# Edge stages of a graph network: sums over groups of 128 edges in place of 256, and a walk table of three rows

## The chip, the cores and the metric

The kernel runs on one core of a Trainium2 chip. The metric is the device time of one execution in microseconds (us). Engines in the text: TensorE (PE; PEld is its weight load), VectorE (DVE), ScalarE (ACT), GpSimd (POOL), SyncE (SP). Line numbers (L1213) are those of the kernel before.

## The reference, cut to what matters

The input is a graph of 6250 nodes with 256 features and 200,000 edges, sorted by their target `dst`. Three graph-attention layers run one after the other. Two other parts, a linear-attention mixer and a mixture of experts, complete the model; the change does not touch them.

```python
xh = (h @ W).reshape(n, heads, d)
a_s = (xh * att_src).sum(-1)
a_d = (xh * att_dst).sum(-1)
alpha = leaky_relu(a_s[src] + a_d[dst], 0.2)
amax = segment_max(alpha, dst, num_segments=n)
e = exp(alpha - amax[dst])
z = segment_sum(e, dst, num_segments=n)
out = segment_sum(xh[src] * (e / z[dst])[:, :, None], dst, num_segments=n)
h = relu(layernorm(out + bias) (+ h))
```

For every edge a row of its source node is fetched, weighed with a softmax over all edges of the same target, and added to the target's row.

## The kernel before, in words

**The walk** (`prepare_walk`) runs once. It cuts the sorted edges into groups and the nodes into 49 blocks of 128 (`NB`). A step of the walk is one pair of a group of edges and a block of nodes: a group whose targets lie in two blocks is visited twice. With groups of 256 edges (`GE`) there are 782 groups (`TG`) and 782 + 48 steps. For each step the walk finds which group it is (`grp`, by counting on TensorE how many groups the walk has passed), fetches the group's targets, the following edge's targets and the sources with three indirect DMAs per 128 steps (L297, L299, L301), and makes from them: `srcT` (source index of every edge), `relT` (the target's place in its block), `lastT`, the masks and links for the segment maximum (`lanes`, `links`), `powers`, and `words`, in which the block numbers of a window are packed.

**Edge stages** (`edge_phase`) run three times, between node stages that compute `rows`, the 260 values per node which the edges fetch. An edge stage goes over windows of `WS` = 20 lanes, and a lane is 128 edges. Before, a window is `WG` = 10 groups of 256 edges, and there are 83 windows (`NW`). The windows are written out one after the other, not looped. What happens to window w is spread over several steps of a software pipeline. In the step n each engine runs a fixed list:

- POOL gathers the 20 lanes of a window, one indirect DMA for 128 edges (L1213), up to four windows ahead (`RING`); before it writes chunk k of a buffer it waits until the sums of that chunk, four windows back, are done.
- PE: sums of window n, between them the `distances` of window n+3; then `spread_fade` (n+1), `turn` (n+2), more sums, `spread_ad` (n+3), the last sum, the mixer's matmuls, and `turn_back` (n+2).
- DVE: `differences` and `tops` (n+1), `sum_ad`, `sum_scores` and `leak` (n+2; `sum_scores`, L1565, waits for the window's last gather), then `fade_sums` and the `add`s of window n (L1684), and between these adds the `weigh`s (L1666) and `onehots` (L1658) of window n+1, and the two scans and what belongs to them for window n+2. `scan_on` (L1579) waits for PE's `turn` and ACT's `fade`.
- ACT: `exponentials` (n+1), five copies of one-hot chunks (n+3, L1263), `fades` (L1251), the mixer's functions, and `load_node` (L1232), which copies one small tile per group.

The sum of a group is two matmuls, one per lane, added up in one PSUM bank; DVE then adds the bank to the block's row of `acc`. Three banks are in use:

```python
wait_past(pe, added, WG * w + g + 1 - since_bank(g))
for j in range(2):
    mm = pe.matmul(ps_o[BANK_OF[g]][:, 0:GW], OH[:, 2 * g + j, :], G[n][:, 2 * g + j, :],
                   start=(j == 0), stop=(j == 1))
mm.then_inc(summed, 1)
```

The add waits for the add before it, as both may go to the same block, and its address comes from a register:

```python
v.wait_ge(summed, WG * w + g + 1)
v.wait_ge(added, WG * w + g)
a = acc[:, bass.ds(b, 1), :].rearrange("p a c -> p (a c)")
v.tensor_tensor(a, a, ps_o[BANK_OF[g]][:, 0:GW], ALU.add).then_inc(added, 1)
```

The block b comes from `blocks_of` (L1106): a word is loaded into a register, and each next block adds one bit of it. The mixer's 49 tiles run beside the first 49 to 55 windows of each edge stage.

## Time and profile before

| what | us |
|---|---|
| median of 3 runs | 7659.41 (7658.97 to 7662.24) |
| the profiled execution | 7658.34 |
| its span, first to last instruction | 7656.4 |
| walk, up to the node stage's first DMA | 124.0 |
| edge stage 0, first to last sum_scores | 2056.5 |
| edge stage 1, the same | 2054.4 |
| edge stage 2, the same | 2055.1 |

The busy time of an engine counts its own instructions, not those of its sequencer (waits, register work). Idle time is put down to what ended it. The rest of the span is node stages, a final stage and the experts.

### The profile page before, as it was taken

What the parts mean: (1) busy time and instruction counts of PE and PEld (TensorE: products, weight loads), DVE (VectorE), ACT (ScalarE), POOL (GpSimd) and SP (SyncE); (2) the same over time, 40 slices, a digit from 0 to 9 for tenths busy, and PEclk for the clock granted to TensorE, in tenths of its full rate; (3) what the DMA queues carried; (4) which work ended last, traced back from release to release, by engine and by line L of the source; (5) the groups of instructions that cost most, each with busy time, mean ns of one, the idle gap of its engine ahead of it and who ended that gap; (6) DMA issues with size and microseconds to landing.
All of it is one profiled execution on the core that took longest, in us unless ns stands there. A gap on an engine that the chain in (4) does not pass through costs nothing. (4 is left out here: it accounts for less than half of the span.)

```text
span 7656.4 us, 113586 instructions
## 1 busy us (share of the span) xinstructions
PE 5492.3 (72%) x23859; PEld 3669.8 (48%) x23860; DVE 5058.0 (66%) x13667; ACT 2558.7 (33%) x7905; POOL 5156.8 (67%) x5441
## 2 busy tenths in 40 slices
PE   3587777777776577777777776577878877673498
PEld 1354454444444355555544444355555544442397
DVE  4466666666667577777776667577777776668643
ACT  1322222222222333334332223244444432223465
POOL 1577777777774677777777773677777777771443
PEclk8777877877767677777777767687787777776699
DMA  4555555554543444444444444444444444444444
GB/s 121 157 145 142 143 145 141 145 139 136 140 138 102 119 120 123 121 123 123 122 116 112 112 110 122 120 123 129 129 126 129 127 119 111 112 110 142 131 71 92
DMA packets 547591, 955.11 MB, mean 125 GB/s; under 512 B 126946, under 2 KB 380876, under 8 KB 546827
## 3 DMA queue, kind: packets, MB, share of 16 engines
q0 software_dynamic: 260256, 692.79, 34.5%
q1 hardware_dynamic: 283451, 253.69, 11.0%
q8 instruction: 177, 2.90, 0.2%
q14 instruction: 411, 3.37, 0.1%
q10 hardware_dynamic: 3296, 2.36, 0.1%
HBM read 801.28 MB, written 155.92 MB: 125 GB/s over the span
## 5 line engine op out<-in xcount | busy, mean ns | idle before, releaser
L1213 POOL DMA_INDIRECT edges_G<-rows,edges_index x4980 | 4721.0, 948 | 1661.9 <-issue 1482.3
L1425 PE MATMUL edges_ps_o<-edges_G,edges_OH 128*128 128x264 f32 x9960 | 3561.9, 508 | 1200.2 <-DVE acc L1684 1197.0
L1425 PEld LDWEIGHTS edges_ps_o<-edges_G,edges_OH 128*128 128x128 f32 x9960 | 2319.0, 250 | 1989.8 <-DVE acc L1684 1367.0
L1263 ACT ACTIVATE edges_OHT<-edges_ps_far 128x512 bf16<-128x512 f32 x1245 | 740.9, 595 | 2299.6 <-PE edges_ps_far L1385 2299.5
L1666 DVE TENSOR_TENSOR edges_G<-edges_G,edges_ps_c 128x1024 f32<-128x1024 f32 x1245 | 1503.2, 1208 | 0.0
L1684 DVE TENSOR_TENSOR acc<-acc,edges_ps_o 128x264 f32 x2490 | 1060.1, 426 | 299.3 <-DVE acc L1684 162.2
L1565 DVE TENSOR_TENSOR edges_tu<-edges_ad,edges_G 128x80 f32<-128x80 f32 x249 | 75.1, 301 | 1255.5 <-DMA edges_G<-rows,edges_index 1255.5
L1385 PE MATMUL edges_ps_far<-edges_rels,pole_rows 5*128 5x512 bf16 x1245 | 618.8, 497 | 344.4 <-ACT edges_OHT L1263 301.8
L1658 DVE TENSOR_TENSOR edges_OH<-edges_ps_c,relT 128x512 f32<-128x512 f32 x1245 | 846.0, 680 | 0.6 <-ACT edges_ps_c L1240 0.5
L1385 PEld LDWEIGHTS edges_ps_far<-edges_rels,pole_rows 5*128 5x128 bf16 x1245 | 117.6, 94 | 976.8 <-issue 497.6
L1232 ACT ACTIVATE edges_node<-terms 128x12 bf16 x2490 | 476.1, 209 | 143.2 <-issue 89.0
L1240 ACT ACTIVATE edges_ps_c<-edges_diff 128x80 f32<-128x80 f32 x249 | 60.0, 241 | 1108.4 <-DVE edges_diff L1646 1107.2
L1579 DVE TENSOR_TENSOR_SCAN edges_run<-edges_masks,edges_ps_s 128x128 f32<-128x128 bf16 x249 | 104.8, 421 | 378.4 <-ACT edges_fade L1251 374.3
L2467 POOL DMA_INDIRECT x<-experts_Y,experts_token x105 | 165.1, 1572 | 252.5 <-DMA x<-experts_Y,experts_token 215.9
L1340 ACT ACTIVATE edges_xh<-edges_R,edges_mshift,edges_mscale 128x256 f32<-128x256 f32 x98 | 58.8, 600 | 574.2 <-DVE edges_mshift L1732 574.2
L2039 POOL DMA_INDIRECT xslot<-final_XH,final_slots x98 | 100.4, 1025 | 173.1 <-DVE final_slots L2219 145.1
L2493 PEld LDWEIGHTS experts_psH<-experts_xs,experts_Wup 128*128 128x128 f32 x1680 | 206.3, 194 | 5.3
L2493 PE MATMUL experts_psH<-experts_xs,experts_Wup 128*128 128x128 f32 x1680 | 206.7, 277 | 0.0
L2502 PE MATMUL experts_psY<-W,experts_hT 128*128 x840 | 198.7, 380 | 0.1
L895 PE MATMUL node_psB<-node_Wx,node_hT 128*128 128x264 f32 x588 | 192.8, 460 | 0.0
L1375 PEld LDWEIGHTS edges_ps_s<-edges_node,edges_OHT 128*128 128x128 bf16 x4980 | 161.2, 96 | 53.0 <-issue 10.9
L1375 PE MATMUL edges_ps_s<-edges_node,edges_OHT 128*128 128x12 bf16 x4980 | 161.9, 168 | 12.3 <-DVE edges_run L1579 10.2
(360 smaller groups left out, 6057.8 us busy)
## 6 DMA issues: line engine op xcount, KB each, us to landing
edges_G<-rows,edges_index POOLq DMA_INDIRECT x4980
xslot<-edges_blank SPq DMA_DIRECT2D x80, 650.0 KB
edges_masks<-lanes SPq DMA_DIRECT2D x249, 96.0 KB
rows<-node_ext SPq DMA_DIRECT2D x147, 130.0 KB, 2.3
experts_X<-xslot SPq DMA_DIRECT2D x105, 130.0 KB, 2.1
node_rows<-rows SPq DMA_DIRECT2D x98, 130.0 KB, 2.2
h<-node_Hn SPq DMA_DIRECT2D x98, 128.0 KB, 1.7
W<-in_L_ffn_W SPq DMA_DIRECT2D x16, 512.0 KB
```

The source lines that it names most:

```text
L895: pe.matmul(psB[slot % 2][:, 0:RW + H], hT[:, slot % TILE_RING, k, :], Wx[:, k, :], start=(k == 0), stop=False)
L1213: g.indirect_dma_start(G[n][:, s, 0:RW], None, dr["rows"], bass.IndirectOffsetOnAxis(index[n][:, s:s + 1], 0)).then_inc(gathered[n], 16)
L1232: ins = a.activation(node[n][:, g, :], terms[:, bass.ds(b, 1), :, :].rearrange("p a h k -> p (a h k)"), ACT.Copy)
L1263: a.activation(OHT[:, 4 * k:4 * k + 4, :].rearrange("p s e -> p (s e)"), ps_far[:, :], ACT.Relu, bias=1.0, scale=-1.0).then_inc(oht_ready, 1)
L1375: mm = pe.matmul(ps_ad[:, s * KEPT:(s + 1) * KEPT], OHT[:, s, :], node[n][:, s // 2, :], start=True, stop=True)
L1385: pe.matmul(ps_far[:, :], pole[r, :], rels[r, 4 * k * P:4 * (k + 1) * P], start=True, stop=True).then_inc(far_ready, 1)
L1425: mm = pe.matmul(ps_o[BANK_OF[g]][:, 0:GW], OH[:, 2 * g + j, :], G[n][:, 2 * g + j, :], start=(j == 0), stop=(j == 1))
L1658: v.tensor_tensor(OH[:, 4 * k:4 * k + 4, :], ps_iota.unsqueeze(1).broadcast_to([P, 4, P]), rel.unsqueeze(2).broadcast_to([P, 4, P]), ALU.i ...
L1666: v.tensor_tensor(g4[:, :, :, 0:D], g4[:, :, :, 0:D], ps_w[:, 4 * k:4 * k + 4, :].unsqueeze(3).broadcast_to([P, 4, H, D]), ALU.mult).then_ ...
L1684: v.tensor_tensor(a, a, ps_o[BANK_OF[g]][:, 0:GW], ALU.add).then_inc(added, 1)
L2493: mm = pe.matmul(psH[slot % 2][:, c * P:(c + 1) * P], Wup[:, slot % 2, k, c * P:(c + 1) * P], xs[:, slot % 2, k, :], start=(k == 0), stop= ...
L2502: mm = pe.matmul(psY[slot % 2][:, 0:C], hT[:, slot % 2, c * P:(c + 1) * P], W2[:, bass.ds(e, 1), c, :].rearrange("p a o -> p (a o)"), star ...
```

## The change

A group becomes one lane of 128 edges. There are now 1563 groups, 1563 + 48 steps of the walk and 81 windows of 20, so 1620 lanes a stage instead of 1660. Each lane has its own matmul pair with start and stop, its own bank in turn, its own add and its own block, taken from two words a window. `load_node` copies 20 tiles instead of 10. The DVE list holds the adds two at a time where it held one, and four between the first two weighs.

The walk is written anew: one DRAM table of three rows per group (targets, following targets, sources) is made straight from the inputs by DMAs on ACT's queue, and one indirect DMA fetches all three rows for 128 steps. The last targets are loaded from the input itself. The group numbers come as a row and are turned by 13 small matmuls. Links, masks and powers go out in 4 DMAs instead of 43, and `powers` lies step by step in DRAM.

```diff
 H = 4
 D = C // H
 RW = C + H
-GE = 2 * P
+GE = P
 GW = RW + H
 TG = -(-E // GE)
-WG = 10
-WS = 2 * WG
-NW = -(-(TG + NB - 1) // WG)
-NG = NW * WG
+WS = 20
+HG = WS // 2
+NW = -(-(TG + NB - 1) // WS)
+NG = NW * WS
 LANES = 32
 POLE = 5
...
+        triples = dr["triples"]
+        sources = ((dst, 0), (dst, 1), (src, 0))
...
+            full = (TC - 1) * P
+            sp.dma_start(dstI[:, 0:TC - 1, :], dst[0:full * GE].rearrange("(c p e) -> p c e", p=P, e=GE)).then_inc(dst_in, 16)
             sp.wait_ge(pool, 1)
-            full = (TC - 1) * P
-            sp.dma_start(dstI[:, 0:TC - 1, :], dr["dst_pad"][0:full, :].rearrange("(c p) e -> p c e", p=P)).then_inc(dst_in, 16)
-            sp.dma_start(dstI[0:pad_rows - full, TC - 1, :], dr["dst_pad"][full:pad_rows, :]).then_inc(dst_in, 16)
+            sp.dma_start(dstI[0:whole - full, TC - 1, :], dst[full * GE:whole * GE].rearrange("(p e) -> p e", e=GE)).then_inc(dst_in, 16)
+            sp.dma_start(dstI[whole - full:whole - full + 1, TC - 1, 0:rest], dst[whole * GE:E].rearrange("(a e) -> a e", a=1)
+                         ).then_inc(dst_in, 16)
...
+        @block.scalar
+        def _(a):
+            for m, (of, o) in enumerate(sources):
+                a.dma_start(triples[0:whole, m, :], of[o:o + whole * GE].rearrange("(t e) -> t e", e=GE)).then_inc(edges_in, 16)
+            for m, (of, o) in enumerate(sources):
+                a.dma_start(triples[whole:TG, m, 0:rest - o], of[o + whole * GE:E].rearrange("(a e) -> a e", a=1)).then_inc(edges_in, 16)
+            a.wait_ge(pads_set, 2)
+            a.dma_start(triples[TG:pad_rows, :, :], pad[:, :, :]).then_inc(edges_in, 16)
+            for m, (of, o) in enumerate(sources):
+                a.dma_start(triples[whole:TG, m, rest - o:P], pad[:, m, rest - o:P]).then_inc(edges_in, 16)
+            a.wait_ge(lanes_ready, 3)
+            a.dma_start(dr["lanes"].rearrange("(c p) x -> p c x", p=P), lanes[:, :, :, :].rearrange("p c m e -> p c (m e)")
+                        ).then_inc(walk_out, 16)
+            a.wait_ge(powers_ready, 3)
+            a.dma_start(dr["powers"].rearrange("(c p) k e -> p c (k e)", p=P), powers[:, :, :, :].rearrange("p c k e -> p c (k e)")
...
+            g.wait_ge(edges_in, 16 * 10)
             g.wait_ge(index_ready, 1)
             for c in range(GC):
-                g.indirect_dma_start(Dg[:, c, :, :].rearrange("p a b -> p (a b)"), None, dr["dst_pad"],
-                                     bass.IndirectOffsetOnAxis(grpI[:, c:c + 1], 0)).then_inc(dst_rows, 16)
-                g.indirect_dma_start(Ng[:, c, :, :].rearrange("p a b -> p (a b)"), None, dr["dst_next"],
-                                     bass.IndirectOffsetOnAxis(grpI[:, c:c + 1], 0)).then_inc(next_rows, 16)
-                g.indirect_dma_start(Sg[:, c, :, :].rearrange("p a b -> p (a b)"), None, dr["src_pad"],
-                                     bass.IndirectOffsetOnAxis(grpI[:, c:c + 1], 0)).then_inc(src_rows, 16)
+                g.indirect_dma_start(Tg[:, c, :, :].rearrange("p a b -> p (a b)"), None, triples.rearrange("t a b -> t (a b)"),
+                                     bass.IndirectOffsetOnAxis(grpI[:, c:c + 1], 0)).then_inc(rows_in, 16)
 
...
+                    v.tensor_copy(st[t][:, c * P:c * P + n], ps_tr[:, c % 3, m * P:m * P + n]).then_inc(copied, 1)
+            v.wait_ge(copied, 3 * GC)
 
         @block.tensor
         def _(pe):
             pe.wait_ge(iotas, 8)
             for c in range(TC):
                 pe.wait_ge(compared, c + 1)
-                for r in range(2):
-                    pe.matmul(ps_row[:, r, 0:rowT], ones[:, :], passed[:, c, r * rowT:(r + 1) * rowT],
-                              start=(c == 0), stop=(c == TC - 1))
-            for m in range(GC):
-                for c in range(TC):
-                    mm = pe.matmul(ps_col[:, m:m + 1], passed[:, c, m * P:(m + 1) * P], ones[:, 0:1],
+                for r in range(QUARTERS):
+                    mm = pe.matmul(ps_row[:, r, 0:rowT], ones[:, :], passed[:, c, r * rowT:(r + 1) * rowT],
                                    start=(c == 0), stop=(c == TC - 1))
             mm.then_inc(walked, 1)
+            pe.wait_ge(row_ready, 1 + QUARTERS)
+            for m in range(GC):
+                mm = pe.matmul(ps_col[:, m:m + 1], row_grp[:, m * P:(m + 1) * P], st["ident"][0:1, 0:1], start=True, stop=True)
+            mm.then_inc(row_turned, 1)
+            pe.wait_ge(index_ready, 1)
+            pe.wait_ge(ends_ready, 2)
+            for m in range(2):
+                mm = pe.transpose(ps_col[0:GC, (1 + m) * P:(2 + m) * P], edge_ends[:, m, :], st["ident"][:, :])
+            mm.then_inc(ends_turned, 1)
             pe.wait_ge(rows_ready, 3)
...
@@ -925,13 +894,12 @@
     srcT, relT, lastT, words = (st[n] for n in ("srcT", "relT", "lastT", "words"))
     pole = st["pole"]
     BANKS = 3
-    BANK_OF = (0, 1, 2, 0, 1, 2, 0, 1, 2, 1)
-    CHUNKS = WG // 2
+    CHUNKS = WS // 4
     KEPT = 3 * H
     with Phase(nc, f"edges{layer}") as ph:
         G = [ph.sb(f"G{r}", [P, WS, GW]) for r in range(RING)]
         index = [ph.sb(f"index{r}", [P, WS], I32) for r in range(RING)]
-        node = [ph.sb(f"node{r}", [P, WG, KEPT], BF16) for r in range(RING)]
+        node = [ph.sb(f"node{r}", [P, WS, KEPT], BF16) for r in range(RING)]
         masks = ph.sb("masks", [P, RING, 1 + 3 * P], BF16)
         links = ph.sb("links", [P, RING, 2, WS], BF16)
...
 
             return not isinstance(i, int) or 0 <= RING * i + n + k < NW
 
-        def since_bank(g):
-
-            return next(d for d in range(1, WG + 1) if BANK_OF[(g - d) % WG] == BANK_OF[g])
+        def bank(w, g):
+            return ps_o[(WS * w + g) % BANKS][:, 0:GW]
 
         def blocks_of(eng, w):
 
-            word = eng.value_load(words[0:1, bass.ds(w, 1)], min_val=0, max_val=64 * 2 ** (WG - 1) - 1)
-            b = eng.snap(word & 63)
-            for g in range(WG):
-                b = nc.s_assert_within(b, 0, NB - 1, skip_runtime_bounds_check_because=ROWS_SEEN)
-                yield b
-                if g < WG - 1:
-                    b = eng.snap(b + ((word >> (6 + g)) & 1))
+            for half in range(2):
+                word = eng.value_load(words[0:1, bass.ds(2 * w + half, 1)], min_val=0, max_val=64 * 2 ** (HG - 1) - 1)
+                b = eng.snap(word & 63)
+                for g in range(HG):
+                    b = nc.s_assert_within(b, 0, NB - 1, skip_runtime_bounds_check_because=ROWS_SEEN)
+                    yield b
+                    if g < HG - 1:
+                        b = eng.snap(b + ((word >> (6 + g)) & 1))
 
         @block.sync
         def _(sp):
@@ -1132,7 +1100,7 @@
                 if w > 1:
                     wait_apart(sp, far_ready, FAR * (w - 1), passed_sp)
                 r = LANES * (w % 2)
-                sp.dma_start(rels[r:r + 3, :], dr["powers"][:, bass.ds(w * WS * P, WS * P)]).then_inc(rels_in[w % 2], 16)
+                sp.dma_start(rels[r:r + 3, :].rearrange("k (v e) -> k v e", e=P), dr["powers"][bass.ds(w * WS, WS), :, :].rearrange("v k e -> k v e")).then_inc(rels_in[w % 2], 16)
 
...
@@ -1372,7 +1340,7 @@
                 wait_past(pe, ad_ready, w)
                 wait_past(pe, ran, w)
                 for s in range(WS):
-                    mm = pe.matmul(ps_ad[:, s * KEPT:(s + 1) * KEPT], OHT[:, s, :], node[n][:, s // 2, :], start=True, stop=True)
+                    mm = pe.matmul(ps_ad[:, s * KEPT:(s + 1) * KEPT], OHT[:, s, :], node[n][:, s, :], start=True, stop=True)
                 mm.then_inc(ad_spread, 1)
 
                 for g in groups:
                     if g == 0:
                         pe.wait_ge(topped, w + 1)
-                    if g % 2 == 0:
-                        pe.wait_ge(oh_ready, CHUNKS * w + g // 2 + 1)
-                        pe.wait_ge(weighed, CHUNKS * w + g // 2 + 1)
-
-                    wait_past(pe, added, WG * w + g + 1 - since_bank(g))
-                    for j in range(2):
-                        mm = pe.matmul(ps_o[BANK_OF[g]][:, 0:GW], OH[:, 2 * g + j, :], G[n][:, 2 * g + j, :],
-                                       start=(j == 0), stop=(j == 1))
-                    mm.then_inc(summed, 1)
+                    if g % 4 == 0:
+                        pe.wait_ge(oh_ready, CHUNKS * w + g // 4 + 1)
+                        pe.wait_ge(weighed, CHUNKS * w + g // 4 + 1)
+
+                    wait_past(pe, added, WS * w + g + 1 - BANKS)
+                    pe.matmul(bank(w, g), OH[:, g, :], G[n][:, g, :], start=True, stop=True).then_inc(summed, 1)
 
             SPLITS = 3 - layer
 
@@ -1497,7 +1462,7 @@
                 here = exists(i, n)
                 for g in range(FAR):
                     if here:
-                        sums(i, n, [g])
+                        sums(i, n, (2 * g, 2 * g + 1))
                     if exists(i, n, 3):
                         distances(*later(i, n, 3), g)
...
@@ -1505,11 +1470,11 @@
                 if exists(i, n, 2):
                     turn(*later(i, n, 2))
                 if here:
-                    sums(i, n, range(5, 9))
+                    sums(i, n, range(10, 18))
                 if exists(i, n, 3):
                     spread_ad(*later(i, n, 3))
                 if here:
-                    sums(i, n, range(9, 10))
+                    sums(i, n, range(18, 20))
                 if mix:
                     mixes(i, n)
...
 
             def onehots(i, n, k):
                 w = RING * i + n
 
-                wait_past(v, summed, WG * (w - 1) + 2 * k + 2)
-                rel = relT[:, bass.ds(w * WG + 2 * k, 2), :].rearrange("p g j -> p (g j)")
+                wait_past(v, summed, WS * (w - 1) + 4 * k + 4)
+                rel = relT[:, bass.ds(w * WS + 4 * k, 4)]
                 v.tensor_tensor(OH[:, 4 * k:4 * k + 4, :], ps_iota.unsqueeze(1).broadcast_to([P, 4, P]),
                                 rel.unsqueeze(2).broadcast_to([P, 4, P]), ALU.is_equal).then_inc(oh_ready, 1)
 
@@ -1669,19 +1634,19 @@
             def fade_sums(i, n, b):
                 w = RING * i + n
                 v.wait_ge(fade_ready, w + 1)
-                wait_past(v, added, WG * w)
+                wait_past(v, added, WS * w)
                 a = acc[:, bass.ds(b, 1), 0:RW].rearrange("p a (h f) -> p (a h) f", h=H)
                 v.tensor_tensor(a, a, fade[:, :].unsqueeze(2).broadcast_to([P, H, D + 1]), ALU.mult).then_inc(faded, 1)
 
             def add(i, n, g, b):
                 w = RING * i + n
-                v.wait_ge(summed, WG * w + g + 1)
+                v.wait_ge(summed, WS * w + g + 1)
                 if g == 0:
                     v.wait_ge(faded, w + 1)
                 else:
-                    v.wait_ge(added, WG * w + g)
+                    v.wait_ge(added, WS * w + g)
                 a = acc[:, bass.ds(b, 1), :].rearrange("p a c -> p (a c)")
-                v.tensor_tensor(a, a, ps_o[BANK_OF[g]][:, 0:GW], ALU.add).then_inc(added, 1)
+                v.tensor_tensor(a, a, bank(w, g), ALU.add).then_inc(added, 1)
 
             def sum_kv(t):
...
                     fade_sums(i, n, b)
                     next(extra, None)
                     add(i, n, 0, b)
+                    add(i, n, 1, next(blocks))
                     next(extra, None)
-                    add(i, n, 1, next(blocks))
+                    for g in (2, 3):
+                        add(i, n, g, next(blocks))
                 if one:
                     weigh(*next1, 0)
                 next(extra, None)
                 if here:
-                    add(i, n, 2, next(blocks))
+                    for g in (4, 5):
+                        add(i, n, g, next(blocks))
                     next(extra, None)
-                    add(i, n, 3, next(blocks))
+                    for g in (6, 7):
+                        add(i, n, g, next(blocks))
                 if one:
                     weigh(*next1, 1)
                     onehots(*next1, 0)
@@ -1804,12 +1773,14 @@
                 if two:
                     scan_on(*next2)
                 if here:
-                    add(i, n, 4, next(blocks))
+                    for g in (8, 9):
+                        add(i, n, g, next(blocks))
                 next(extra, None)
                 if two:
                     scan_back(*next2)
                 if here:
-                    add(i, n, 5, next(blocks))
+                    for g in (10, 11):
+                        add(i, n, g, next(blocks))
                 if two:
                     turn_edges(*next2)
...
```

The parts left out rename semaphores and tiles of the walk, drop the second lane's index from its tiles, and repeat the pairing of the adds to the end of the list.

## Rows read from the trace of the kernel before

**Rows 1.** The page, part 1: busy time, share of the span and instructions of each engine.

```profile
PE 5492.3 (72%) x23859; PEld 3669.8 (48%) x23860; DVE 5058.0 (66%) x13667; ACT 2558.7 (33%) x7905; POOL 5156.8 (67%) x5441
```

**Rows 2.** Windows of the three stages, POOL's L1213: the row of their sum.

```profile
sum 6165.94, POOL 4660.16; mean POOL 1553.39
```

**Rows 3.** The page, part 5: xcount | busy, mean ns of one | idle before, releaser.

```profile
L1213 POOL DMA_INDIRECT edges_G<-rows,edges_index x4980 | 4721.0, 948 | 1661.9 <-issue 1482.3
...
L1425 PE MATMUL edges_ps_o<-edges_G,edges_OH 128*128 128x264 f32 x9960 | 3561.9, 508 | 1200.2 <-DVE acc L1684 1197.0
...
L1684 DVE TENSOR_TENSOR acc<-acc,edges_ps_o 128x264 f32 x2490 | 1060.1, 426 | 299.3 <-DVE acc L1684 162.2
```

**Rows 4.** Waits of DVE: 780:1481, 3050:3751, 5343:6044, 1684:2260, whole span (us, times, longest).

```profile
DVE edges_tu L1565 <- DMA edges_G<-rows,edges_index: 140.7, 28, 6.2
...
DVE edges_tu L1565 <- DMA edges_G<-rows,edges_index: 134.6, 29, 5.7
...
DVE edges_tu L1565 <- DMA edges_G<-rows,edges_index: 107.4, 28, 5.2
...
DVE edges_tu L1565 <- DMA edges_G<-rows,edges_index: 118.0, 23, 6.2
...
DVE edges_run L1579 <- ACT edges_fade L1251: 374.3, 242, 2.3
```

**Rows 5.** Timeline of DVE, stage 0: start us, us, instruction, [idle before <-releaser].

```profile
1308.69 0.43 DVE L1684 TENSOR_TENSOR acc<-acc,edges_ps_o 128x264 f32 x1
1309.85 0.43 DVE L1684 TENSOR_TENSOR acc<-acc,edges_ps_o 128x264 f32 x1 [0.73 <-DVE acc L1684]
1310.20 1.22 DVE L1666 TENSOR_TENSOR edges_G<-edges_G,edges_ps_c 128x1024 f32<-128x1024 f32 x1
```

**Rows 6.** Timeline of DVE, end of stage 0: the second to the fourth of ten adds.

```profile
2369.98 0.43 DVE L1684 TENSOR_TENSOR acc<-acc,edges_ps_o 128x264 f32 x1 [0.38 <-PE edges_ps_o L1425]
2370.79 0.43 DVE L1684 TENSOR_TENSOR acc<-acc,edges_ps_o 128x264 f32 x1 [0.38 <-DVE acc L1684]
2371.59 0.43 DVE L1684 TENSOR_TENSOR acc<-acc,edges_ps_o 128x264 f32 x1 [0.37 <-DVE acc L1684]
```

**Rows 7.** L1106 by source: times in ns, min/median/max.

```profile
L1106 DVEq TENSOR_LOAD <-words x249: 299/303/559, 329.2 to 6927.8; - x125
L1106 DVEq FUSED_REGOPS  x249: 190/197/210, 329.8 to 6928.1; - x125
```

**Rows 8.** Timeline of PE, stage 0, one window.

```profile
1311.76 2.13 PE L1425 MATMUL edges_ps_o<-edges_G,edges_OH 128*128 128x264 f32 x4
1313.83 0.60 PE L1385 MATMUL edges_ps_far<-edges_rels,pole_rows 5*128 5x512 bf16 x1
...
1321.29 1.16 PE L1425 MATMUL edges_ps_o<-edges_G,edges_OH 128*128 128x264 f32 x4 [0.59 <-DVE acc L1684]
1322.28 0.39 PE L1466 MATMUL edges_ps_r<-edges_v,edges_high 128*128 128x130 f32 x2
...
1324.89 0.27 PE L1401 MATMUL edges_ps_s<-ident,edges_greatest 128*128 128x128 f32 x1
```

**Rows 9.** Timeline of ACT, the same window.

```profile
1315.43 0.26 ACT L1251 ACTIVATE edges_fade<-edges_ps_s,edges_front 128x4 f32<-128x4 f32 x1 [0.37 <-PE edges_ps_s L1393]
...
1317.32 2.41 ACT L1232 ACTIVATE edges_node<-terms 128x12 bf16 x10 [0.49 <-issue]
```

**Rows 10.** Timeline of the walk, all engines.

```profile
10.19 0.41 SPq L231 DMA_DIRECT2D walk_dstI<-dst_pad  x1
...
21.79 5.01 PE L405 MATMUL walk_ps_row<-walk_passed,walk_ones 128*128 128x415 bf16 x14 [21.79 <-DVE walk_passed L328]
...
28.79 1.16 POOL L297 DMA_INDIRECT walk_Dg<-dst_pad,walk_grpI  x1 [23.67 <-DVE walk_grpI L332]
...
96.23 16.46 SPq L263 DMA_DIRECT2D links<-walk_links  x28
124.03 0.34 SPq L573 DMA_DIRECT2D node_X<-in_x  x1
```

More of the change, by code:

```diff
@@ L354, in _ @@
-            ch.add(v.tensor_copy(Nf[:, :, :, :], Ng[:, :, :, :]))
-            v.tensor_copy(Sf[:, :, :, :], Sg[:, :, :, :]).then_inc(rows_ready, 1)
-            ch.wait()
-            for c in range(GC):
-                ch.add(v.tensor_scalar(rel[:, c, :, :], Df[:, c, :, :], blk[:, c:c + 1], float(2 * P - 1), ALU.subtract, ALU.min))
-            ch.wait()
-            v.tensor_scalar(rel[:, :, :, :], rel[:, :, :, :], -1.0, None, ALU.max).then_inc(rows_ready, 1)
-            v.tensor_tensor(last[:, :, :, :], Df[:, :, :, :], Nf[:, :, :, :], ALU.not_equal).then_inc(rows_ready, 1)
@@ L1823, in step @@
                 if here:
-                    add(i, n, 6, next(blocks))
+                    for g in (12, 13):
+                        add(i, n, g, next(blocks))
                 if two:
@@ L1827, in step @@
                 if here:
-                    add(i, n, 7, next(blocks))
+                    for g in (14, 15):
+                        add(i, n, g, next(blocks))
                 if two:
@@ L1839, in step @@
                 if here:
-                    add(i, n, 8, next(blocks))
+                    for g in (16, 17):
+                        add(i, n, g, next(blocks))
                 if one:
@@ L1843, in step @@
                 if here:
-                    add(i, n, 9, next(blocks))
+                    for g in (18, 19):
+                        add(i, n, g, next(blocks))
                 for _ in extra:
```

228 lines of the change are left out of this document (94 added, 134 removed).

## The prediction

> **What bounds the kernel now.** I began with the page's busy shares [rows 1]: TensorE, VectorE and GpSimd are busy for two thirds to three quarters, so they don't tell which one sets the pace. The stretches of the three edge stages do [rows 2]. From the first to the last sum_scores (L1565) the stages take 6165.94 us for 3 x 82 windows: 25.06 us a window. POOL's gathers [rows 3] are 20 a window, 0.948 us each with 0.30 us of issue between two (1482.3 us over 4980), 20 x 1.25 = 25.0 us. So GpSimd's gathers are the period, in all three stages.
>
> VectorE is next. In each window it stands still at sum_scores until the window's last gather has landed [rows 4]: 140.7/28 = 5.0 us a window in the part of stage 0 that also mixes, 134.6/29 = 4.6 in stage 1, 107.4/28 = 3.8 in stage 2, 118.0/23 = 5.1 once the 49 mixing tiles are done. Taken from 25.06 that leaves VectorE's own path: 20.0, 20.4, 21.2 and 19.9 us. This slack, 3.8 to 5.1 us, is what the change may spend for nothing.
>
> **Fewer windows.** 256-edge groups give 782 + 48 = 830 groups, 83 windows of 10. 128-edge groups give 1563 + 48 = 1611, so 81 windows of 20. Two windows a stage go, 40 gathers: if the period stayed, 6 x 25.06 = 150 us less.
>
> **Ten more adds a window.** A window still has 20 pairs of matmuls, but every one ends its own sum, so the add to acc (L1684) comes 20 times instead of 10. One add is 426 ns [rows 3], but its price depends on its neighbour. Behind an add, an independent instruction starts 0.35 us later (1309.85 to 1310.20), while an add behind an add starts far later, with the idle time put down to acc itself [rows 5]. It waits for the add before it, and then its block address is worked out. At the stage's end ten stand in a row, the second to the fourth at 2369.98, 2370.79 and 2371.59: 0.80 us apart, 0.38 of it idle [rows 6]. The new order puts the adds in pairs and, between weigh 0 and weigh 1, in a four. Each of the ten new ones has another add just in front, so I take 10 x 0.80 = 8.0 us. Bounds: 10 x 0.35 = 3.5 if their waits cost nothing, and 10 x 1.16 = 11.6 by the slowest pair shown (1308.69 to 1309.85).
>
> The Trainium skill ("VectorE: DVE Perf Modes", section "The DRAIN you can't avoid") speaks against this price: eight copies with a semaphore after each took as long as eight with one at the end, so a semaphore costs nothing extra there. By that rule the ten adds cost little over 3.5 us. The trace disagrees for this dependent add: 0.80 against 0.35 us [rows 5, 6].
>
> **The second word of blocks.** Twenty blocks need two words, so before add 10 there is a second load and decode on VectorE's sequencer: 0.303 + 0.197 = 0.50 us [rows 7]. scan_back, and the wait for add 9, cover part. I take 0.3 us a window, bounds 0 and 0.6.
>
> **What TensorE and ScalarE do to VectorE then.** scan_on waits for the fade, on average 374.3/242 = 1.55 us a window [rows 4]. The fade comes from PE behind sums and distances. Before, PE needed only add 1 for the last distance; now it needs add 6 (three banks, and sum 9 is in front of distance 4). From add 6 to the fade PE has about one sum, a distance, the fade matmul and a transpose. At the slow clock that is 1.07 (2.13 for two sums), 1.60 from the last distance's start to the fade's (1313.83 to 1315.43) and the fade's own 0.26: 2.9 us. At the fast clock a sum is 0.58 (1.16 for two) [rows 8, 9]. VectorE arrives there about 2.4 us after add 6 (add 7, a 1.13 us weigh, a 0.6 us one-hot). If sum 7 and distance 3 are still queued, another 2 us come on top. I keep half of the wait: -0.8 us; bounds: -1.55 (all gone) and +1.0.
>
> At the step's end, sum 19 needs add 16, and behind it on PE stand the mixes and turn_back, for which the next step's differences wait. From the start of the mixes at 1322.28 to turn_back at 1324.89 are 2.6 us [rows 8], plus a sum before and 0.27 after: 3.5 us. VectorE has add 17, weigh 4, two adds and a one-hot in that time, also about 3.5 us. I take 0.3 us where the window mixes and none later; bounds 0 and 1.5.
>
> **The edits with no price.** ScalarE copies 20 node blocks instead of 10: 2.41 us more a window [rows 9], of an engine busy for 33% of the span [rows 1], and the copies come last in its step; if that idle time went, 2.4 us would stand ahead of the next exponentials. The powers now come as 60 pieces of 256 bytes, not 3 rows: SP asks for them a window ahead. OH, weigh, gathers and matmuls stay 20 a window.
>
> **The new period.** Own path + 8.0 + 0.3 - 0.8 + 0.3 gives 27.8 us in stage 0, 28.2 in stage 1, 29.0 in stage 2. Where nothing mixes it is 19.9 + 8.0 + 0.3 - 0.8 = 27.4. All are over 25.06: VectorE becomes the bound, the 4 us of slack are gone, and POOL waits for sums.
>
> Per stage there are 80 periods after: two before any add, at 25.06, then 49 mixing and 29 without. Sum over stages: 49 x (27.84 + 28.22 + 29.02) = 4169; 3 x 29 x 27.43 = 2386; 6 x 25.06 = 150; together 6706. Before: 6166. That is +540. Behind the last sum_scores three steps with adds remain, which no gather covered before: 3 x 3 x (8.0 - 0.8) = +65.
>
> **The walk.** Before, it ends at 124.03 [rows 10]. Its chain: copies to DRAM until SP's load of dst at 10.19, the search, 21 gathers from 28.79 on, VectorE's work on the tables, then 28 small DMAs on SP from 96.23 (16.46 us) whose last landing the end awaits. After: dst is loaded at once (-9). The search is longer, 52 matmuls for 14 that took 5.01 us, so +14 at 0.36 us each, and some 2 us of turning the row. Only 13 gathers follow, -10 us at 1.25. VectorE casts three tables less, -3. The 28 DMAs become 2 and go out earlier, about -24 with their landing. The sum is -32 us; bounds -50 and -5, as the copies of the table now run beside the load of dst, and no row shows that.
>
> **Sum.** The profiled execution took 7658.34 us (span 7656.4 and 1.9 around it), 1.1 less than the median. 7658.3 + 540 + 65 - 32 = 8231; I say **8230 us**, 7% slower.
>
> **Rivals.**
> *A, the gathers stay the bound.* The new adds find cover, as the skill's rule would have it: 10 x 0.35 = 3.5 us is under the slack of 3.8 to 5.1, the period stays 25.06; it decides below 0.38 to 0.5 us for each added add. Then 7658 - 150 (six windows) + 32 (nine uncovered last steps of 3.5) - 32 = 7508 us. For it: an instruction that isn't an add does start 0.35 us behind one [rows 5]. Against it: [rows 6]. Chance 0.10.
> *B, the ring of three banks.* With one sum a bank PE runs three matmuls ahead, no longer six. If PE stays at the slow clock because it stops at so many adds, sum 7, distance 3 and sums 8 and 9 come in series behind add 4 and hold scan_on back 2.1 us, and the mixes come 1.2 us late. The period is then up 2.4 us from mine: 8230 + 234 x 2.4 = 8790 us. For it: PE already waited 1197 us for acc [rows 3], and after such a wait two sums took 2.13 us instead of 1.16 [rows 8]. Against it: PE had a wait of 5 us there, which VectorE's own wait for gathers made, and that wait goes. Chance 0.08.
>
> **Numbers.** Mine 0.80, A 0.10, B 0.08, and 0.02 for something between the old time and mine. The range: 0.95 us less a period over 234 periods (most of the fade's wait gone) gives 8008, 1.2 us more 8511; 8000 to 8520. Less than 0.2% either way is no change that can be told here. Faster is A, 0.10; same 0.01, from what lies between; slower 0.89.
>
> **What would show it.** Right: sum_scores no longer waits for a gather; the tables show POOL idle for about 2.5 us a window, released by ps_o; 4860 adds of about 0.43 us, second ones 0.8 us behind the first; periods of 27.4 to 29.0 us, the longest in stage 2; the node stage starts near 92 us. Wrong: a period of 25.0 with sum_scores still waiting for gathers (A), or scan_on and the adds waiting for PE for over 4 us a window (B). If the second of a pair starts under 0.5 us after the first, the price of the add is the step that failed.

## The result and the profile after

The changed kernel took **8515.07 us** (8503.82 to 8519.34, 4 runs) beside 7659.19 for the kernel before (7658.87 to 7662.24): a ratio of 1.1115, 95% interval 1.1100 to 1.1131. It is 856 us slower; the forecast was 571 slower (8230) in a range of 8000 to 8520. The direction and the bound that changes were right. A third of the added time was not foreseen, and the time lies inside the range by only 5 us.

The page after, part 1 and the lines that answer to [rows 1, 3]: xcount | busy, mean ns of one | idle before, releaser.

```profile
PE 6287.8 (74%) x23459; PEld 3582.0 (42%) x23460; DVE 6025.0 (71%) x15855; ACT 3055.0 (36%) x10215; POOL 5029.6 (59%) x5312
...
L1181 POOL DMA_INDIRECT edges_G<-rows,edges_index x4860 | 4602.5, 947 | 2545.6 <-issue 2078.7
L1392 PE MATMUL edges_ps_o<-edges_G,edges_OH 128*128 128x264 f32 x9720 | 4322.9, 566 | 1613.5 <-DVE acc L1649 1593.9
...
L1649 DVE TENSOR_TENSOR acc<-acc,edges_ps_o 128x264 f32 x4860 | 2076.0, 427 | 1358.4 <-DVE acc L1649 849.9
```

A gather costs what it did (947 ns), but the idle time before POOL's gathers went from 1661.9 to 2545.6 us. The add costs what it did too (427 ns). There are 2370 more of them, and the idle time in front of them grew from 299.3 to 1358.4 us. This idle time, 1059 us more, and the adds' own busy time, 1016 us more, together use up the 4 to 5 us a window in which VectorE had waited for gathers, and then lengthen the window. The busy shares hide it: DVE shows 71%.

VectorE's waits after, whole span (us in total, times, longest), to be held against [rows 4]:

```profile
DVE acc L1649 <- DVE acc L1649: 849.9, 2224, 0.7
DVE acc L1649 <- PE edges_ps_o L1392: 412.5, 757, 1.6
DVE edges_run L1544 <- ACT edges_fade L1219: 201.5, 147, 2.4
...
DVE edges_diff L1611 <- PE edges_ps_s L1369: 142.8, 87, 3.3
...
DVE edges_tu L1530 <- DMA edges_G<-rows,edges_index: 70.7, 6, 12.9
...
DVE edges_xh L1703 <- ACT edges_ps_c L1208: 31.3, 29, 1.1
...
DVE edges_den L1662 <- ACT edges_ps_c L1208: 30.4, 41, 1.1
```

sum_scores (now L1530) waited for a gather in every window; now it does so 6 times in the whole kernel. In its place stand five waits: the add for the add before it, the add for its sum, scan_on (L1544) for the fade, the differences (L1611) for turn_back, and, in the last two rows, the mixer's first instruction of a step for ScalarE's exponentials (L1208). The first needs no other engine. The next three come from TensorE, the fade by way of ScalarE. The last, 61.7 us in all, doesn't occur in the kernel before: there VectorE's wait for the gathers gave ScalarE the time.

VectorE's timeline in stage 0, as [rows 5]: start us, us, instruction, [idle before <-releaser].

```profile
1299.81 0.43 DVE L1649 TENSOR_TENSOR acc<-acc,edges_ps_o 128x264 f32 x1
1300.62 0.43 DVE L1649 TENSOR_TENSOR acc<-acc,edges_ps_o 128x264 f32 x1 [0.38 <-DVE acc L1649]
1301.43 0.43 DVE L1649 TENSOR_TENSOR acc<-acc,edges_ps_o 128x264 f32 x1 [0.38 <-DVE acc L1649]
1302.23 0.43 DVE L1649 TENSOR_TENSOR acc<-acc,edges_ps_o 128x264 f32 x1 [0.37 <-PE edges_ps_o L1392]
1302.58 1.21 DVE L1631 TENSOR_TENSOR edges_G<-edges_G,edges_ps_c 128x1024 f32<-128x1024 f32 x1
```

Adds behind adds start 0.80 to 0.81 us apart; the weigh behind the last starts after 0.35. So the dependent add has the price that the forecast took from [rows 6]. For eight copies the Trainium skill ("VectorE: DVE Perf Modes", section "The DRAIN you can't avoid") says that a semaphore after each costs nothing extra. This trace disagrees for the dependent add, 0.80 against 0.35 us.

Windows of the three stages, first to last sum_scores, POOL alone (us, busy, PEclk, DMA share, GB/s), as [rows 2]:

```profile
241.58:2546.91 2305.33, 1510.81 (x1595) 0.68 0.44 123
2788.90:5090.22 2301.32, 1510.31 (x1596) 0.73 0.38 103
5356.05:7735.44 2379.39, 1510.75 (x1596) 0.72 0.38 102
sum 6986.04, POOL 4531.87; mean POOL 1510.62
```

6986.04 against 6165.94 us: +820 for 240 periods instead of 246. From the last sum_scores of a stage to the first of the next it is 28.4 and 27.6 us more than before, and 21.9 more to the end: +78. The first sum_scores comes 37 us earlier. Together 820 + 78 - 37 = 861, which is the difference of the spans (8517.2 and 7656.4).

The periods, in the mean of the windows, with the same of the kernel "banks of pairs" below (us):

| windows | forecast | changed kernel | banks of pairs |
|---|---|---|---|
| mixing, stage 0 | 27.8 | 29.0 | 26.6 |
| mixing, stage 1 | 28.2 | 29.6 | 28.1 |
| mixing, stage 2 | 29.0 | 30.9 | 28.5 |
| the rest, stages 0, 1, 2 | 27.4 | 28.9, 27.8, 28.2 | 26.5, 26.7, 26.7 |

TensorE in the same stage, pieces of its timeline:

```profile
1311.37 2.13 PE L1392 MATMUL edges_ps_o<-edges_G,edges_OH 128*128 128x264 f32 x4 [0.29 <-DVE acc L1649]
1314.85 3.01 PE L1392 MATMUL edges_ps_o<-edges_G,edges_OH 128*128 128x264 f32 x6 [1.36 <-DVE acc L1649]
...
1320.34 0.71 PE L1392 MATMUL edges_ps_o<-edges_G,edges_OH 128*128 128x264 f32 x2 [0.87 <-DVE acc L1649]
...
1323.60 1.06 PE L1392 MATMUL edges_ps_o<-edges_G,edges_OH 128*128 128x264 f32 x4
```

The granted clock of these four stretches (us; busy and count of PE and PEld; PEclk, DMA share, GB/s):

```profile
1311.37:1313.50 2.13, 2.12 (x4) 1.07 (x4) 0.50 0.52 168
1314.85:1317.86 3.01, 3.01 (x6) 1.65 (x6) 0.50 0.42 115
1320.34:1321.05 0.71, 0.71 (x2) 0.29 (x2) 1.00 0.33 100
1323.60:1324.66 1.06, 1.06 (x4) 0.58 (x4) 1.00 0.36 114
```

TensorE does a few sums, stops for an add, does a few more. Two sums take 2.13 us at a granted clock of 0.50 (its lower level, 1.2 GHz) and 1.06 us at 1.00 (2.4 GHz), after the mixes, where it had run without a stop. A stop alone doesn't settle the level: the sum at 1320.34 also stands behind one and runs at 1.00. 9720 matmuls were busy for 4322.9 us, 9960 for 3561.9 before; the mean granted clock of the whole run is 0.72 against 0.75.

### The profile page after: what moved, and what is told of

Read it like the earlier page. It is cut to its first block and busy times, and to the rows that moved or that the text cites. A ratio compares the mean times of both kernels' runs of the same rounds, so it can differ in the third digit from the quotient of the medians.

```text
span 8517.2 us, 134431 instructions
## 1 busy us (share of the span) xinstructions
PE 6287.8 (74%) x23459; PEld 3582.0 (42%) x23460; DVE 6025.0 (71%) x15855; ACT 3055.0 (36%) x10215; POOL 5029.6 (59%) x5312
## 5 line engine op out<-in xcount | busy, mean ns | idle before, releaser
L1181 POOL DMA_INDIRECT edges_G<-rows,edges_index x4860 | 4602.5, 947 | 2545.6 <-issue 2078.7
L1392 PE MATMUL edges_ps_o<-edges_G,edges_OH 128*128 128x264 f32 x9720 | 4322.9, 566 | 1613.5 <-DVE acc L1649 1593.9
L1392 PEld LDWEIGHTS edges_ps_o<-edges_G,edges_OH 128*128 128x128 f32 x9720 | 2120.6, 258 | 3255.0 <-DVE acc L1649 2600.0
L1649 DVE TENSOR_TENSOR acc<-acc,edges_ps_o 128x264 f32 x4860 | 2076.0, 427 | 1358.4 <-DVE acc L1649 849.9
L1631 DVE TENSOR_TENSOR edges_G<-edges_G,edges_ps_c 128x1024 f32<-128x1024 f32 x1215 | 1467.4, 1208 | 0.0
L1231 ACT ACTIVATE edges_OHT<-edges_ps_far 128x512 bf16<-128x512 f32 x1215 | 723.6, 596 | 1953.9 <-PE edges_ps_far L1353 1953.8
L1200 ACT ACTIVATE edges_node<-terms 128x12 bf16 x4860 | 979.6, 211 | 347.8 <-issue 225.7
L1623 DVE TENSOR_TENSOR edges_OH<-edges_ps_c,relT 128x512 f32<-128x512 f32 x1215 | 825.3, 679 | 2.8 <-ACT edges_ps_c L1208 2.6
L1208 ACT ACTIVATE edges_ps_c<-edges_diff 128x80 f32<-128x80 f32 x243 | 58.6, 241 | 1462.4 <-DVE edges_diff L1611 1461.5
L1544 DVE TENSOR_TENSOR_SCAN edges_run<-edges_masks,edges_ps_s 128x128 f32<-128x128 bf16 x243 | 101.7, 419 | 219.8 <-ACT edges_fade L1219 201.5
L1343 PEld LDWEIGHTS edges_ps_s<-edges_node,edges_OHT 128*128 128x128 bf16 x4860 | 183.7, 106 | 99.7 <-issue 68.7
L2567 DVE TENSOR_TENSOR experts_Yb<-experts_psY,experts_b 128x256 f32<-128x256 f32 x105 | 44.6, 425 | 166.0 <-PE experts_psY L2477 166.0
```

The lines of the kernel that those rows point to most:

```text
L1181: g.indirect_dma_start(G[n][:, s, 0:RW], None, dr["rows"], bass.IndirectOffsetOnAxis(index[n][:, s:s + 1], 0)).then_inc(gathered[n], 16)
L1200: ins = a.activation(node[n][:, g, :], terms[:, bass.ds(b, 1), :, :].rearrange("p a h k -> p (a h k)"), ACT.Copy)
L1231: a.activation(OHT[:, 4 * k:4 * k + 4, :].rearrange("p s e -> p (s e)"), ps_far[:, :], ACT.Relu, bias=1.0, scale=-1.0).then_inc(oht_ready, 1)
L1343: mm = pe.matmul(ps_ad[:, s * KEPT:(s + 1) * KEPT], OHT[:, s, :], node[n][:, s, :], start=True, stop=True)
L1392: pe.matmul(bank(w, g), OH[:, g, :], G[n][:, g, :], start=True, stop=True).then_inc(summed, 1)
L1623: v.tensor_tensor(OH[:, 4 * k:4 * k + 4, :], ps_iota.unsqueeze(1).broadcast_to([P, 4, P]), rel.unsqueeze(2).broadcast_to([P, 4, P]), ALU.i ...
```

## The experiments

Theories: **D**, VectorE is bound by its chain of dependent adds, 0.80 us each. **P**, TensorE is late, because three banks with one sum each let it run only three sums ahead, and its clock is low. The ratios are against the kernel before, run beside each kernel on the same chip. There were three series of runs; in the first, the kernel before itself took 9099 us (the last section looks at that).

### Ten adds again

```
-  return ps_o[(WS * w + g) % BANKS][:, 0:GW]
+  return ps_o[(HG * w + g // 2) % BANKS][:, 0:GW]
-  pe.matmul(bank(w, g), ..., start=True, stop=True).then_inc(summed, 1)
+  mm = pe.matmul(bank(w, g), ..., start=(g % 2 == 0), stop=(g % 2 == 1))   # then_inc for odd g
   (one add for each pair, one word of blocks loaded)
```

> The changed kernel, but two lanes share one sum and one add again (10 adds a window, banks of two lanes, block numbers of the first word only; so the sums of odd lanes go to the block of another lane: that part of the result is left out). Walk, 81 windows, ScalarE's 20 node copies and the powers in 60 pieces stay as changed. Theory A (the ten added adds, 0.80 us each on VectorE, are what the period grew by): the gathers bound it again at 25.06 us, 243 windows, so 7659 - 150 - 37 = about 7470 us. Rival W (the node copies, the powers or the masks in their new form hold the stages back): it stays above 7900 us.

> The ten adds of the kernel before (pairs of sums in one bank), with everything else of the change; it leaves out the block of every second group. It is the first run again, because ScalarE's node copies lost some 7 us of a window there. D: with ten adds the gathers set the period again, 25.06, and 243 windows instead of 249 and the shorter walk give 7659 - 150 - 37 = 7470, a ratio of 0.975. A window part that neither the adds nor their banks explain would keep it above 1.0.

In the first series the kernel before itself ran at 9098.7 us (7 runs), and this one at 8971.46: ratio 0.9861 (0.9841 to 0.9881). In the third series: **7479.58 us** beside 7660.65, ratio 0.9764 (0.9748 to 0.9780); D had said 7470. VectorE's waits in the later run:

```profile
DVE edges_tu L1533 <- DMA edges_G<-rows,edges_index: 1192.2, 240, 13.3
DVE edges_run L1547 <- ACT edges_fade L1219: 372.5, 236, 2.3
```

The wait for gathers is back in 240 of 243 windows and the three stages take 3 x 2005 us, 25.06 a window. So everything else in the change (128-edge groups, the new walk, 20 node copies, the powers in 60 pieces) brings 181 us, where the forecast had -150 and -32. The loss is in what this kernel takes back: the ten more sums and adds, and the second word of blocks.

### Twenty adds, but banks of pairs

```
-  wait_past(pe, added, WS * w + g + 1 - BANKS)
+  if g % 2 == 0: wait_past(pe, added, WS * w + g + 2 - 2 * BANKS)
   (banks of pairs as above, but each of the two adds reads its pair's bank)
```

> The changed kernel with 20 adds a window as now, but TensorE sums two lanes into one bank, and VectorE adds each bank twice (the separate sums of the two lanes are left out). TensorE may so run six matmuls ahead of the adds, as before the change, not three. VectorE's list is the same. Theory D (the depth of the ring: TensorE at its slow level can't stay ahead of paired adds with one sum a bank, which is the 1.2 us a window that the forecast lacks): about 8230 us, mean period 27.8. Rival S (TensorE's own time at the slow level, not how far it is ahead): above 8430 us.

> Twenty adds as in the changed kernel, but every bank holds the sums of a pair, as before, so that TensorE may run twelve sums ahead instead of six (each bank's contents are added twice, to two blocks). D: adds 0.80 apart stand in full, TensorE's lateness goes: the forecast's own periods, about 28.0, 8230 us, ratio 1.075. P: as much or more goes, with all that hangs on TensorE's clock: the period no longer follows the clock, and the ratio is 1.06 to 1.08. If the bank depth is worth nothing it stays at 1.11.

(BANKS is 3: the second text should say six sums ahead instead of three.) First series: 9353.03 us, ratio 1.0281 (1.0260 to 1.0301). Third series: **8069.35 us**, 1.0533 (1.0516 to 1.0551), under both theories' bands. With it the loss splits: 8069.35 - 7479.58 = **590 us for ten more adds** and the second word, and from there to the changed kernel's 8509.82 in the second series **440 us for the banks**. The edit lets TensorE run further ahead and also has it stop at half as many places; no run separates the two. VectorE's waits:

```profile
DVE acc L1652 <- DVE acc L1652: 887.0, 2330, 0.9
DVE acc L1652 <- PE edges_ps_o L1393: 210.4, 531, 0.9
```

The acc-to-acc wait hardly changed; half of the wait for sums went, and scan_on's wait for the fade (201.5 us in the changed kernel) and the differences' (142.8) are no longer in the list. Of the 2845 adds that stand directly behind an add, the sum of what exceeds 0.80 us is 133 us in the changed kernel and 33 here; almost all of the difference is at one place, add 6. All waits of the adds together are 127 us less, the fade's 202 and the differences' 143 less, while the mixer's wait for the exponentials grew by 44 (61.7 to 105.6). That is 428 us of the 449 between the two profiled executions.

TensorE's lateness goes with its clock. Windows after the mixing tiles, first two of the changed kernel (stages 0 and 1), then two of this one (us; busy and count of PE, PEld, DVE, ACT, POOL; PEclk, DMA share, GB/s):

```profile
1850.00:2510.00 660.00, 527.15 (x1550) 262.81 (x1550) 472.71 (x1150) 182.81 (x684) 428.57 (x453) 0.61 0.44 121
4400.00:5050.00 650.00, 489.80 (x1619) 240.73 (x1619) 493.64 (x1204) 194.51 (x716) 446.86 (x473) 0.73 0.38 102
```

```profile
1700.00:2330.00 630.00, 487.71 (x1649) 287.99 (x1649) 494.90 (x1213) 190.19 (x714) 451.44 (x476) 0.66 0.48 133
4200.00:4780.00 580.00, 446.05 (x1523) 263.56 (x1523) 459.97 (x1125) 175.95 (x659) 413.86 (x436) 0.67 0.40 105
```

The program is the same in both stretches of a fence. At a granted clock of 0.61 the changed kernel does 453 gathers in 660 us (20 in 29.1 us), at 0.73 it does 473 in 650 (27.5). With banks of pairs it is 26.5 and 26.6 us, at 0.66 and 0.67, a step too small to test anything. Window by window, with each stage taken in a mixing and a later part, the changed kernel's period falls by 9 to 18 us for one whole unit of clock (correlation -0.66 to -0.85). In the second trace of it five of the six parts agree, and one shows nothing. With banks of pairs four of six parts show nothing, and in the kernel before the period doesn't move (25.0 to 25.1 us). A correlation doesn't say which drives which: a low clock makes TensorE late, and a TensorE that does less may be granted less, for which the kernel with half the columns speaks (0.568, further down). No run sets the clock by itself, so that half of theory P is not shown.

### The changed kernel, beside its edits

> The changed kernel itself, beside the edits of it. Theory D (VectorE is bound by twenty adds, each behind the one before) and rival P (TensorE, at its slow clock level, is late behind banks that now hold one sum) both say 8515 us and a ratio of 1.11 where the kernel before runs at 7659. Where the kernel before runs at 9099, as in the four runs above, the 7 us that ScalarE's node copies then lose in a window stand in both kernels and cover part of the adds: between 1.05 (the 1.0595 of the kernel with both words loaded together, plus or minus 0.01) and 1.07.

8509.82 us beside 7660.26, ratio 1.1109 (1.1091 to 1.1128). It is the reference for the next three, run in the same series.

### The address worked out ahead of the waits

```
 def add(i, n, g, b):
     w = RING * i + n
+    b = v.snap(v.to_reg(b), min_val=0, max_val=NB - 1)
```

> Every add works out its block register before its waits, so that one register instruction less stands between the end of the add before and its own start. D: adds that follow each other come 0.65 us apart instead of 0.80; if all 20 of a window gain 0.15, the period falls by 3.0 us and the time by 243 x 3.0 = 730 us (ratio to the changed kernel 0.914); if only the 10 that stand directly behind an add gain, by 365 us (0.957). P: the adds only wait longer for their sums; under 120 us (above 0.986).

8273.32 us, ratio 1.0808 (1.0790 to 1.0826): 236 us less than the changed kernel, which neither theory had (D 365 or 730, P under 120). The timeline shows about the spacing that was expected, 0.63 to 0.64 us:

```profile
1302.35 0.42 DVE L1650 TENSOR_TENSOR acc<-acc,edges_ps_o 128x264 f32 x1
1302.98 0.43 DVE L1650 TENSOR_TENSOR acc<-acc,edges_ps_o 128x264 f32 x1 [0.21 <-DVE acc L1650]
```

The acc-to-acc wait fell from 854 to 421 us, and the adds' wait for sums rose from 398 to 501, the fade's from 184 to 264. Between the semaphore and the add stood three register instructions; two of them now run ahead of it, worth 0.16 us a pair, and TensorE took back some two fifths (103 + 80 of 433 us).

### The adds spread out

```
+  W(0); adds(1); O(0); adds(2); next(extra, None); adds(3)
+  W(1); adds(4); next(extra, None); adds(5)
+  W(2); adds(6); O(1); adds(7); next(extra, None)
+  T(scan_on); adds(8); T(scan_back); adds(9); T(turn_edges); adds(10)
+  ...            (W weigh, O one-hot; then to adds(19) in the same way)
```

> The same twenty adds, but between any two of them stands, where the window has one, a weigh, a one-hot or a scan, whose run covers the add's register instructions. D: the 10 adds that followed an add directly cost about 0.45 instead of 0.80, so 3.5 us of a period go, 850 us of the whole down to the gathers' own pace of 25.06: ratio to the changed kernel 0.90 to 0.93. P: the sums come no earlier and the adds are asked for later, so nothing or a loss of up to 100 us (0.99 to 1.012).

7939.12 us, ratio 1.0361 (1.0343 to 1.0378), that is 0.933 of the changed kernel: 571 us less with the same instructions in another order. P had no gain in this run and falls as the whole reason. D's 0.90 to 0.93 was just missed, and the waits say why:

```profile
DVE edges_run L1544 <- ACT edges_fade L1219: 569.3, 237, 3.2
DVE acc L1649 <- DVE acc L1649: 209.7, 559, 0.7
```

The acc wait fell by 645 us, and the fade's rose by 386: VectorE now reaches scan_on before TensorE has the fade.

### Both causes removed, in three steps

One kernel of the second series adds the early address, both words loaded together, and a new order on TensorE and ScalarE; in the third series, one is the same without the new order, and one has the mixes last.

```
-  for half in range(2): word = eng.value_load(...)
+  pair = [eng.value_load(...) for half in range(2)]
+  if g == 2: spread_fade(...); turn(...)       # PE; were behind the last distance
-  five one-hot copies, fade                    # ACT
+  three one-hot copies, fade, two one-hot copies
-  sums 10..17, spread_ad, sums 18, 19, mixes, turn_back
+  sums 10..13, spread_ad, sums 14, 15, mixes, sums 16..19, turn_back
```

> Spread adds, early block registers, both words loaded together, TensorE's order as in the changed kernel. The spread alone gave 1.036, the early registers alone took 0.030 off. D: both gains act on the same register instructions, so they don't add: 1.02 to 1.03. P: then TensorE's order is what the run with everything removed besides (1.0024): the fade wait, 570 us in the spread kernel, stays at 400 or more here.

> Spread adds, early block registers, both words loaded together, and on TensorE the mixes ahead of the last four sums. D and P together (each holds a part): with both removed the gathers set the period again at 25.06, so 243 x (29.1 - 25.06) = 980 us go: ratio to the changed kernel 0.885, and to the kernel before 0.98 (7530 beside 7659). If something third holds the window, it stays above 1.0 of the kernel before.

Without the new order 7744.69 us, 1.0110 (1.0091 to 1.0129), better than the 1.02 to 1.03 that was expected, and the wait for the fade is the same as in the spread kernel, 568.3 us. The adds' wait for each other fell once more, from 209.7 to 109.1 us. With the new order **7676.64 us**, 1.0024 (1.0014 to 1.0034); expected was 7530. The two engines' orders were changed together, so neither has a price of its own. Something third held part of the windows:

```profile
DVE acc L1656 <- PE edges_ps_o L1395: 442.8, 673, 2.3
...
DVE edges_tu L1536 <- DMA edges_G<-rows,edges_index: 133.7, 45, 13.3
```

These are VectorE's waits. The fade's is gone, but the add of group 16 now waited 1.88 us, in the mean of 40 windows of the last stage, for a sum behind the mixes. The last kernel puts them behind the sums and turn_back:

```
-  sums 14, 15, mixes, sums 16..19, turn_back
+  sums 14..19, turn_back, mixes
```

> The kernel with everything removed (1.0024), but TensorE does the mixes after the last sum and after the turned drops. There the add of group 16 waited 1.88 us in a window of the last stage's mixes. If that wait goes and nothing takes its place, the mixing windows fall from 25.4, 25.9 and 27.3 to the gathers' 25.06 or to 25.4: 50 x (0.3 + 0.9 + 1.9) = 155 us less, 7520 us, ratio 0.982. If TensorE, at its slow level, is then late with the first sums of the next window instead, it stays between 1.0 and 1.01.

**7593.81 us**, ratio 0.9914 (0.9898 to 0.9931): below both kernels, the kernel before by 0.9%. 7520 was not reached, and VectorE's waits tell where the rest is:

```profile
DVE acc L1654 <- PE edges_ps_o L1395: 310.0, 693, 1.4
DVE edges_tu L1534 <- DMA edges_G<-rows,edges_index: 205.1, 106, 13.2
DVE acc L1643 <- issue: 177.5, 243, 1.3
```

The gathers set 106 windows. The mixing windows still take 25.15, 25.6 and 26.1 us in the three stages, against 25.06. The last row was 30.6 us in the changed kernel: loading both words together stands 0.7 us a window in front of the multiply by the fade (L1643), the window's first instruction on acc. It bought little: in the spread kernel add 10, behind the second word's load, had been idle for 137 us in all, and with both words together 4, while 147 us came in front. No run undoes this edit alone.

### Two that tell little

```
 halfcols:  pe.matmul(bank(w, g)[:, 0:GW // 2], OH..., G[n][:, g, 0:GW // 2], ...)
 word:      both words of a window loaded together
```

> The changed kernel with sums of 132 instead of 264 columns (the other half of each sum is left out; the banks are zeroed once). TensorE's work for the sums is about halved, VectorE's stays. Theory A alone (VectorE's own chain is all of the period, 29.2 us): no change, 8510 us. Theory A with TensorE (D or S: what goes beyond 27.2 us is waiting for sums): windows of 27.0 to 28.5 us everywhere, about 8150 us.

> The changed kernel; the second word of block numbers is loaded right behind the first, not before add 10. In the trace add 10 starts 1.25 us after scan_back, idle 0.84 us. Theory L (this load is on VectorE's path in every window): 0.5 us less a window, 8390 us. Rival: it is hidden behind waits for TensorE in the slow windows and shows only in the fast ones: 8450 to 8490 us.

Half the columns: 9497.17 us, 1.0439 (1.0418 to 1.0460); both words: 9638.62, 1.0595 (1.0577 to 1.0613), beside 9098.7. The changed kernel wasn't run there, so neither has its reference, and the word load has no price of its own; in its trace the wait in front of the multiply by the fade is 177.9 us, as in the last kernel (177.5). Shorter sums didn't make TensorE punctual in proportion: its mean granted clock was 0.568 (0.677 with both words loaded together), and a sum's matmul took 476 ns on average against 593, for half the columns.

## Why the prediction was right, and by how much not

*What bounds it.* Right: slack used up, POOL idle behind VectorE, period over 25.06 in all stages and longest in stage 2. The periods, though, are 27.8 to 30.9 us where 27.4 to 29.0 was given. Of POOL's idle time the profile puts 322 us, 1.3 a window, down to ps_o, not 2.5; most of the increase stands as "issue" (1482.3 to 2078.7 us).

*Windows and walk.* Forecast -150 and -32 (the walk's own terms add up to -30), measured 181 together by the kernel with ten adds. That the two agree to a microsecond is in part luck, as the walk itself was off: the node stage's first load came at 82.24 instead of 124.03, 10 us earlier than forecast. Some 7 of these are the search, whose 52 row sums were done sooner:

```profile
12.02 12.73 PE L372 MATMUL walk_ps_row<-walk_passed,walk_ones 128*128 128x405 bf16 x52 [12.02 <-DVE walk_passed L305]
...
82.24 0.37 SPq L542 DMA_DIRECT2D node_X<-in_x  x1
```

12.73 us for 52, where 0.36 each had made 19. By the first sum_scores, 37 us of the 42 are left.

*Ten adds at 0.80.* Right in kind and size. With banks of pairs the period was 26.5 to 26.7 where nothing mixes; the forecast's terms with all of the fade's wait gone, its own lower bound, give 19.9 + 8.0 + 0.3 - 1.55 = 26.65.

*The mis-sized step: what TensorE and ScalarE do to VectorE then.* The sum had two terms for it, half of the fade's wait kept and 0.3 us at turn_back, and none for the adds' waits for their sums. The fade was right (190 us forecast as 243 x 0.78, 201.5 measured). At turn_back 44 us were forecast and 142.8 measured; as forecast it stood in mixing windows (138 of the 142.8), but at 0.9 us each, not 0.3. The adds waited 412.5 us for sums; an add behind an add stands 0.38 us anyway, so 757 x 0.38 = 288 of these were paid already and some 125 are new. The count over adds that directly follow an add gives the same 125 (133 us over 0.80, 8 before the change). ScalarE's exponentials had no term and cost 62. The second word was priced too high, if anything: in front of the add behind scan_back VectorE stood 61 us before the change and 93 after, where the forecast had 61 + 73, so 41 less. 99 + 125 + 62 - 41 = 245 of the 280 us by which the stages passed the forecast (820 against 540). The other 35 us are open.

*Rival B* named this mechanism and gave it 0.08. The banks cost 440 us over the kernel with banks of pairs; the forecast stood 161 us above that kernel (8230 - 8069) and B 721. The truth lay about halfway. So the forecast is right in what bounds the kernel and in the adds' price, and B's mechanism holds beside it; that 8515 still fell under 8520 is luck, since the range's upper end, 1.2 us more a window, for which the forecast gives no reason, just covers the 1.2 us that were missing. B's own threshold, over 4 us a window, wasn't reached: sums and fade made (412.5 + 201.5) / 243 = 2.5. What was missed is not the mechanism, since B names the stops at many adds, but its weight: it went into the sum only at the fade and at turn_back, and beyond that all or nothing, with 0.08 for its full size.

*Tail steps.* +65 forecast, +78 measured.

## What to carry to other kernels

Price a dependent instruction by its start-to-start distance in a row of like ones (0.80 us here), not by its duration (0.43), and look first whether other work can stand between two of them: reordering alone gave back 571 of 850 us. When a buffer holds half as much per slot, price the producer's lateness in every consumer of it, also in those queued behind it on the producer's engine (here the fade and turn_back, 344 us together). Removing one wait moves the next one up, on engines that nobody had looked at too (ScalarE's exponentials, 62 us here): four of the edits here (early address, spread, all together, mixes last) gave less than their own terms, and moving the mixes on the producer gave 83 us more at the end.

## What the runs showed of the hardware that was not expected

The same kernel (ten adds) took 8971 us in the first series and 7480 in the third, and the kernel before 9099 in the first and 7660 in the second, both times on the same chip. In the kernel with ten adds the difference stands in ScalarE's node copies. First the earlier run's timeline of ScalarE, then the later one's:

```profile
1516.10 0.21 ACT L1200 ACTIVATE edges_node<-terms 128x12 bf16 x1 [0.71 <-issue]
1518.29 0.21 ACT L1200 ACTIVATE edges_node<-terms 128x12 bf16 x1 [1.97 <-issue]
1522.05 0.21 ACT L1200 ACTIVATE edges_node<-terms 128x12 bf16 x1 [3.55 <-issue]
```

```profile
1504.42 2.41 ACT L1200 ACTIVATE edges_node<-terms 128x12 bf16 x10 [0.33 <-issue]
```

The copy costs 0.21 us in both. Between copies stand register instructions that take 0.04 us (median); in the earlier run 1953 of them took over 0.6, none in the later one, and 20 copies took 15.7 us on average instead of 5.2. In the kernels with twenty adds of that series VectorE's register instructions came late too (919 over 0.6 us with banks of pairs, 613 with half the columns, 146 with both words together), which makes comparisons within the first series loose as well. The page's idle time before them was 2920.0 us against 352.5. Why the instructions came late there is open. It is a reason to run both the kernel before and the changed kernel beside every experiment.

An add behind another through one accumulator costs 0.80 us with three register instructions behind the wait and 0.64 with one, both at 0.43 us of busy time.
